# A graph network's message blocks: values woven in pairs of slots, one reduction for the maximum, and another order of the blocks

## The reference

```
msg     = relu(h[src] + edge_attr) + 1e-7
m       = msg * t
seg_max = segment_max(m, dst)
ex      = exp(m - seg_max[dst])
denom   = segment_sum(ex, dst)
agg     = segment_sum(msg * ex / denom[dst], dst)
out     = mlp(h + agg)          # 64 -> 128 -> layer norm -> relu -> 64
```

## Time and profile before

| | |
|---|---|
| median of 3 runs | 5808.66 us |
| the profiled execution, its span | 5825.41 us, 5823.0 us |
| busy in the span: PE, DVE, POOL, ACT | 81%, 78%, 69%, 34% |
| first gather of each layer at | 1686.0, 2708.5, 3732.3, 4757.7 us |
| mean granted TensorE clock | 0.868 of full |

### The profile page before, as it was taken

How to read it: one execution, slowest core, us unless ns; L and a number is a source line. 1 busy time by engine, 2 the same in 40 slices (tenths; PEclk the granted TensorE clock), 3 DMA queues, 4 the chain that set the end, 5 groups by cost and what they waited for, 6 DMA issues and landing times.

```text
span 5823.0 us, 108077 instructions
## 1 busy us (share of the span) xinstructions
PE 4692.3 (81%) x43853; PEld 3246.1 (56%) x43853; DVE 4557.1 (78%) x8649; ACT 1992.2 (34%) x3506; POOL 4032.3 (69%) x3659
## 2 busy tenths in 40 slices
PE   6727788899958888886888798688888867896887
PEld 6726677788945554553555455355545544554544
DVE  9723555654549998996999899699989968997887
ACT  3314675665523332332233223223323322222222
POOL 2433777777637777774777777477777747777775
PEclk8966987976659999998999999899999978998988
DMA  8993777775665556554555655455565545555552
GB/s 338 413 304 111 274 282 270 263 274 211 240 218 196 183 198 181 186 200 144 181 186 200 174 192 193 148 173 198 191 174 200 184 148 177 188 189 161 177 178 96
DMA packets 317390, 1192.47 MB, mean 205 GB/s; under 512 B 139314, under 2 KB 142564, under 8 KB 249556
## 3 DMA queue, kind: packets, MB, share of 16 engines
q1 hardware_dynamic: 166676, 920.68, 42.9%
q0 software_dynamic: 128800, 209.18, 14.0%
q10 hardware_dynamic: 21408, 55.60, 2.4%
HBM read 930.35 MB, written 254.82 MB: 204 GB/s over the span
## 4 chain that ended last, share of the span: by engine, by line
DVE 35%; PE 13%; POOL 10%; issue 8%; DMA 2%; ACT 2%; SPq 0%; DVEq 0%; POOLq 0%
POOL gb L1285 9%; PE bank L1394 9%; DVE ep_layers L1384 5%; DVE xb L1318 5%; DVE ep_layers L1345 5%; DVE ep_layers L1370 4%; DVE ep_layers L1340 4%; PE bank L1302 2%; DMA gb<-ztab,ovi 2%; DVE xb L1328 1%; DVE ds L1404 1%; DVE na L1431 1%; ACT hb L282 1%; DVE st L254 1%; PE bank L1448 1%
## 5 line engine op out<-in xcount | busy, mean ns | idle before, releaser
L1285 POOL DMA_INDIRECT gb<-ztab,ovi x2512 | 2794.2, 1112 | 869.5 <-issue 736.3
L1394 PE MATMUL bank<-ep_layers,keep 128*128 128x512 f32 (+3 forms) x4928 | 2248.6, 616 | 43.2 <-DVE ep_layers L1384 43.2
L1394 PEld LDWEIGHTS bank<-ep_layers,keep 128*128 128x128 f32 x4928 | 995.9, 205 | 1241.1 <-issue 1181.8
L1302 PE MATMUL bank<-zpw,oh_layers 128*128 128x64 bf16 x28812 | 880.8, 194 | 104.2 <-DMA zpw<-ztab 104.1
L1302 PEld LDWEIGHTS bank<-zpw,oh_layers 128*128 128x128 bf16 x28812 | 874.4, 98 | 159.0 <-issue 137.1
L1131 POOL DMA_INDIRECT ecell<-zpw,ptg x588 | 627.3, 1067 | 227.8 <-issue 175.6
L1376 ACT ACTIVATE ep_layers<-ep_layers,pack 128x1280 f32<-128x1280 f32 (+14 forms) x484 | 641.9, 1347 | 190.1 <-DVE ep_layers L1370 183.9
L1370 DVE SCALAR_TENSOR_TENSOR ep_layers<-xb,bank 128x1280 f32<-128x1280 f32 (+14 forms) x484 | 689.2, 1468 | 6.8
L1384 DVE SCALAR_TENSOR_TENSOR ep_layers<-xb,ep_layers 128x1280 f32<-128x1280 f32 (+14 forms) x484 | 687.0, 1469 | 0.4
L960 PE MATMUL bank<-byk,zpw 96*102 96x102 f32 (+13 forms) x4608 | 624.3, 317 | 43.2 <-DVE zpw L941 39.4
L960 PEld LDWEIGHTS bank<-byk,zpw 96*102 96x102 f32 (+13 forms) x4608 | 609.4, 224 | 58.5 <-DVE zpw L941 49.2
(11 more groups left out here) (219 smaller groups left out, 4697.2 us busy)
## 6 DMA issues: line engine op xcount, KB each, us to landing
oh_layers<-ohd SPq DMA_DIRECT2D x196, 1568.0 KB
cb<-rowc SPq DMA_DIRECT2D x49, 1152.0 KB
ea_in<-in_ea SPq DMA_DIRECT2D x101, 512.0 KB, 9.3
enc<-es_out ACTq DMA_DIRECT2D x101, 512.0 KB
gb<-ztab,ovi POOLq DMA_INDIRECT x2512
ohd<-oh_lay SPq DMA_DIRECT2D x49, 736.0 KB
xb<-ecell SPq DMA_DIRECT2D x20, 1536.0 KB
xb<-ecell SPq DMA_DIRECT2D x20, 1504.0 KB
```

The costliest lines, as they stand in the source:

```text
L1285: at["g"][d] = ga_l[d % GB_BLOCKS](GP.indirect_dma_start(gb[:, c:c + 64], None, from_rows, bass.IndirectOffsetOnAxis(ap=ovi[:, i:i + 1], a ...
L1302: q = PE.matmul(gps[j % n_gp][:, 64 * (s % 8):64 * (s % 8) + 64], oh[:, d % 2, at_oh:at_oh + 128], zp[:, b, 64 * part:64 * part + 64], sta ...
L1394: q = PE.matmul(both[:, 0:w], ident, rows[:, 128 * (c - a):128 * (c - a) + w], start=(c == 0), stop=(c + 4 >= S.S[d]), skip_group_check=True)
```

## The change

1. A new tile `xs` ("woven" in the profile) takes the sums of `add` and `over`, instead of `xb`. Slot pairs are interleaved in it: features of a slot q of half 0 and a slot q of half 1 stand next to each other (`half(t, a, b)` is one of the two, with a step of two elements). `over` is cut in two where it crosses the halves; where S is odd a memset fills the missing slot.
2. `most` is one `tensor_reduce` over pairs and slots, into `mx`, and one `tensor_scalar` (maximum with 0) into `top_x`; ACT applies its own relu before its exp for `cm`.
3. `sub` and `mul` read `xs`, in slices that each lie in one half, of at most 28 slots. One block has four slices, and its fourth `sub` comes behind its first `mul`. `xb` is free after `over`, and `add(d, 0)` waits for the last `mul`.
4. The order: V = 7, 6, 6, 5, then 13, 16, 13, 15, 13, 15, 12 ... 13, 11, 36, 11, 21, 11, 20, 10, 19 ... 16, 9, 16, 9, and 8, 8, 8, 7 at the end. The block of 36 stands at place 25, and its `gb_after` is 24. `prepare` scatters nodes by their plain rank and reads them back with five strided DMAs, instead of computing the places with nine small operations.

```diff
-        self.turn = self.ND // 2
-        ends = [d // 2 if d % 2 else self.ND - 1 - d // 2 for d in range(self.ND)]
-        self.sorted = ends[self.turn:] + ends[:self.turn]
+        few, half = self.ND - 8, (self.ND - 9) // 2
+        self.runs = [(0, 1, few + 4, 4), (4, 2, half, few - half), (5, 2, half // 2, half - half // 2),
+                     (5 + 2 * (half - half // 2), 2, 0, half // 2), (self.ND - 4, 1, few, 4)]
+        at = {p + step * i: b + i for p, step, b, n in self.runs for i in range(n)}
...
+            def half(t, a, b):
+                return xs[:, 128 * a:128 * b].rearrange("p (q f t) -> p t q f", t=2, f=64)[:, t]
...
-                k["add"][d] = V(VE.tensor_tensor(x, gps[j % n_gp][:, 0:64 * (hi - lo)], x,
-                                                 ALU.add))
+                if j == 0 and "read" in link:
+                    vwait(link["read"])
+                t, q = place[j]
+                k["add"][d] = V(VE.tensor_tensor(
+                    half(t, q, q + hi - lo), by_slot(gps[j % n_gp][:, 0:64 * (hi - lo)]),
+                    by_slot(x_of(d, lo, hi)), ALU.add))
...
-                q = V(VE.tensor_tensor(row[:, 0:64 * m], x_of(d, 0, m), x_of(d, n - m, n), ALU.max))
-                yield
-                while m > 2:
-                    vwait(q)
-                    w = m // 2
-                    q = V(VE.tensor_tensor(row[:, 0:64 * w], row[:, 0:64 * w],
-                                           row[:, 64 * (m - w):64 * m], ALU.max))
-                    m -= w
...
-                q = k["topx"][d] = V(VE.scalar_tensor_tensor(
-                    top, row[:, 0:64], 0.0, row[:, 64:128], ALU.max, ALU.max))
-                vwait(q)
-                q = k["topx"][d] = V(VE.tensor_copy(top_x[:, d % 2, :], top))
+                q = V(VE.tensor_reduce(top, xs[:, 0:128 * halves(d)[0]].rearrange(
+                    "p (q f t) -> p f q t", t=2, f=64), AX.XY, ALU.max))
+                yield
+                vwait(q)
+                q = k["topx"][d] = V(VE.tensor_scalar(top_x[:, d % 2, :], top, 0.0,
+                                                      None, ALU.max))
...
                 for i in range(n):
                     mul(d, i)
+                    if i + EP_SLICES < n:
+                        sub(d, i + EP_SLICES)
```

More of the change, by code:

```diff
@@ L62, in __init__ @@
         assert self.ones[-1] == self.ND and self.G == 36
-        self.turn = self.ND // 2
-        ends = [d // 2 if d % 2 else self.ND - 1 - d // 2 for d in range(self.ND)]
-        self.sorted = ends[self.turn:] + ends[:self.turn]
+        few, half = self.ND - 8, (self.ND - 9) // 2
+        self.runs = [(0, 1, few + 4, 4), (4, 2, half, few - half), (5, 2, half // 2, half - half // 2),
+                     (5 + 2 * (half - half // 2), 2, 0, half // 2), (self.ND - 4, 1, few, 4)]
+        at = {p + step * i: b + i for p, step, b, n in self.runs for i in range(n)}
+        self.sorted = [at[d] for d in range(self.ND)]
+        assert sorted(self.sorted) == list(range(self.ND))
         self.place = [self.sorted.index(b) for b in range(self.ND)]
@@ L1248, in x_of, with by_slot, halves @@
                 return xb[d % 2][:, 64 * a:64 * b]
-            def slices(d):
-                n = -(-S.S[d] // EP_SLOTS)
-                w = 4 * -(-S.S[d] // (4 * n))
-                return [(a, min(S.S[d], a + w)) for a in range(0, S.S[d], w)]
+            def half(t, a, b):
+                return xs[:, 128 * a:128 * b].rearrange("p (q f t) -> p t q f", t=2, f=64)[:, t]
+            def by_slot(t):
+                return t.rearrange("p (q f) -> p q f", f=64)
+            place = [(0, 0), (0, 8), (1, 0), (1, 8), (0, 16)]
+            def halves(d):
+                return -(-S.S[d] // 2), S.S[d] // 2
+            def slices(d):
+                cuts = []
+                for t, m in enumerate(halves(d)):
+                    n = -(-m // EP_SLOTS)
+                    w = 4 * -(-m // (4 * n)) if n > 1 else m
+                    cuts += [(t, a, min(m, a + w)) for a in range(0, m, w)]
+                return cuts
             ring_of, ring_user = {}, []
@@ L1261, in ring @@
                 return ring_of[d, i] % EP_SLICES
-            def wait_ring(d, i):
-                n = ring_of[d, i]
-                if n >= EP_SLICES:
-                    VE.wait_ge(pe_s, k["sums"][ring_user[n - EP_SLICES]])
             def load_x(d):
@@ L1326, in over @@
                 awaits(VE, at["g"][d])
-                x = x_of(d, G, S.S[d])
-                k["over"][d] = V(VE.tensor_tensor(x, gb[:, 64 * S.gb_at[d]:64 * (S.gb_at[d] + S.V[d])], x, ALU.add))
+                row = gb[:, 64 * S.gb_at[d]:64 * (S.gb_at[d] + S.V[d])]
+                m = halves(d)[0] - 20
+                for t, q, a, b in ((0, 20, 0, m), (1, 16, m, S.V[d])):
+                    if b > a:
+                        k["over"][d] = link["x_free"][d % 2] = V(VE.tensor_tensor(
+                            half(t, q, q + b - a), by_slot(row[:, 64 * a:64 * b]),
+                            by_slot(x_of(d, G + a, G + b)), ALU.add))
+                if S.S[d] % 2:
+                    m = halves(d)[1]
+                    V(VE.memset(half(1, m, m + 1)[:, 0], 0.0))
             def most(d):
-                vwait(max(k["over"][d], k["add"][d]))
+                vwait(V.n)
                 top = mx[:, 64 * (d % 2):64 * (d % 2) + 64]
@@ L1380, in mul @@
             def mul(d, i):
-                a, b = slices(d)[i]
+                t, a, b = slices(d)[i]
                 r = ring(d, i)
                 VE.wait_ge(ae_s, k["exp"][d, i])
-                k["mul"][d, i] = link["x_free"][d % 2] = V(VE.scalar_tensor_tensor(
-                    ep[:, r, 0:b - a, 64:128],
-                    x_of(d, a, b).rearrange("p (s f) -> p s f", f=64), 0.0,
-                    ep[:, r, 0:b - a, 0:64], ALU.max, ALU.mult))
+                k["mul"][d, i] = link["read"] = V(VE.scalar_tensor_tensor(
+                    ep[:, r, 0:b - a, 64:128], half(t, a, b), 0.0, ep[:, r, 0:b - a, 0:64],
+                    ALU.max, ALU.mult))
                 PE.wait_ge(ve_s, k["mul"][d, i])
@@ L1394, in mul @@
                     q = PE.matmul(both[:, 0:w], ident, rows[:, 128 * (c - a):128 * (c - a) + w],
-                                  start=(c == 0), stop=(c + 4 >= S.S[d]),
+                                  start=(i == 0 and c == a),
+                                  stop=(i == len(slices(d)) - 1 and c + 4 >= b),
                                   skip_group_check=True)
@@ L1613, in layer @@
                 steps(99, "end" if ready else "turned")
-                for i in range(1 if ready else 0, n):
+                for i in range(1 if ready else 0, min(n, EP_SLICES)):
                     sub(d, i)
```

54 lines of the change are left out of this document (18 added, 36 removed).

## The result

The changed kernel takes 5985.07 us (median of 4 runs, 5975.22 to 5987.5) and the one before 5811.2 (5808.57 to 5826.21): 1.0291 times as long, 95% interval 1.0269 to 1.0312. I had forecast 5736. The profiled execution took 5987.5, its span is 5985.1.

The account below looks back on a forecast made before the run. DVE and POOL were taken to run level, both full and coupled through delayed gathers. Layer terms of -4, -14, -14 and -41 us made -73, so 5808.7 - 73 = 5736 us, range 5685 to 5835.

Parts of the forecast that it names:

- The maximum: In `most` on DVE: one reduction and a small operation take 3.51 us instead of 4.42, saving 44.6 us a layer.
- DVE's work: DVE's net change over a whole layer, from the shorter reduction, additions, slices and waits for PE: -30 us a layer.
- The block with four slices: Its fourth `sub` must wait for PE's sums behind its first `mul`: +4.4 us a layer on DVE.
- What POOL gets back: Gathers on POOL, no longer delayed by the tree of maxima, get back 60 us a layer, bounds 0 and 75.
- the first rival: The reduction delays POOL's gathers as long as the tree did, so POOL gets nothing back: 5861 us, chance 0.09.
- What is added on DVE: Split `over`, memset and two new waits on DVE cost 0.23 us a block, 11 a layer.
- hand-offs: First `add` waiting for last `mul`, 0.06 us, and reduction waiting for everything before, 0.05; bounds 0 and 0.2 each.
- The order: New block order changes DVE's waits for gathers by +26, +16, +16 and -11 us in the four layers.
- start waits: First two `over` of a layer wait 3.98 and 5.77 us; fewer early gathers save 9.7 in layers two and three.
- the pairs cost POOL what they cost DVE, +3: Behind the block of 36, alternating blocks of about 20 and 10 gathers cost only 3 us.
- the waits that exist grow, +5: DVE's existing waits for PE grow 5 us a layer, as the shorter maximum takes 0.9 of 2 us slack.
- What would show it wrong: Wait at block of 36 above 45 us or missing, gathers staying at 1.1 us, or DVE awaiting PE every block.

## Why the prediction was wrong

I had forecast 73 us less; it became 174 us more. The runs at full pace make a table: medians in us, those of before 5810.73 to 5818.51 in the same jobs.

| | order of before | new order |
|---|---|---|
| tree, its own steps | 5811 to 5819 (before) | 5967.81 |
| woven, two steps | 5696.8 | 5848.09 |
| woven, one step | 5828.46 | 5985.07 (the change) |

Each part has about the same price wherever the table has it twice: the woven tile and reduction -122 and -120, the order +151 to +157, the lost step +132 and +137. -122 + 151 + 137 = +166, measured +174. The lost step beside the tree has no run at full pace.

- **The maximum.** The size was right: 3353 ns for 3072 columns, forecast 3.35 us. The way to it was partly luck. I called the two rows of my slope contiguous, but `fold` (684 ns for 512 columns) adds four sums that lie 128 columns apart in PSUM; the contiguous row alone (1953 ns for 1728, 1.13 a column) would have given 3.47. I had forecast DVE's work at -30 us a layer; its busy time is down by 27 in the second layer and 30 in the last. The woven tile with its reduction, by itself, is worth 120 to 122 us of time.
- **The block with four slices** waits 29.6 us over four layers, forecast 17.6.
- **What POOL gets back.** The mean of a gather is 1042 ns, forecast near 1.02, so 70 of 1112 - 940 = 172 ns: 44 us a layer instead of 60. The direction holds: the first rival fell. What it is worth in time no run separates.
- **The step that failed first: "What is added on DVE"**. I counted the instructions that the change adds and not what it takes from the schedule around them. `most` is a place where the node stage is issued, and with the second yield gone one cast on ACT moved behind an exp. Nothing in the rows of before shows such a wait (4.4 us in 12 times). The nearest term of the forecast is that for hand-offs, 11 us a layer within 0 and 30, and it stood for other waits; the lost step costs 137 us, and its waits are all in the three layers that write rows, 44.6 us in each.
- **The step that failed second: "The order"**. I priced it by gathers alone: +26, +16, +16 and -11 us of waits, 47 in all. That part came, near enough: waits for gathers are 147.0 us where those figures add up to 37 + 37 + 37 + 54 = 165, with 34.8 us at the block of 36 (forecast 33) and none of the start waits. But the order's price is 151 us. Between the two kernels with two steps the waits show where: +74 for linear2, +50 for gathers, +26 for the rows of the residual input, together 150. I had written "the pairs cost POOL what they cost DVE, +3" and "the waits that exist grow, +5" for PE, and never asked which of a pair's two blocks the residual add follows. The place costs 132 us in the new order (up to 36 of them can be the block of 36) and 32 in the order of before, where only 11 pairs have it and the two blocks of a pair differ less on the whole. With the places right in both (and the block of 36 two places ahead in the new order), the new order costs 5716 - 5665 = 51 us more, close to the 47 that I had for it (by the waits 36 for gathers and 18 for the residual rows): the gathers were priced near enough, the pair was not priced at all. The wait of `h` for linear2, 31.1 us in 29 times, was in the trace of before.
- **The sum.** -73 was made of -120, +47 and nothing for the other two. With the measured 137 for the step and 151 for the order it would have been -120 + 137 + 151 = +168.
- **What would show it wrong.** "If DVE waits for PE in every block" came true in kind: DVE waits for linear2 88 times in 100 node units, that is in nearly every pair of blocks. PE's waits at `fold` stayed below the 25 us, read as a layer's like the figures around it: 43.7 us in four layers, 10.7 in the second where before has 14.1. PE's longer leg showed at linear2 and not where I looked for it.
- **The layers.** The first lost 71 us, the second and third 52 and 50, the last gained 7. In each of the first three the cast wait grew by 43 us and the wait for linear2 by 28 to 30. The first layer's waits for gathers grew by 24 us and the second's by 14, since the first had no start waits to lose, as forecast; that is 10 of the 19 us between them. In the last layer there is no cast wait, and waits for gathers fell from 64.7 to 41.8 us, forecast 54.

## What to carry to other kernels

Where instructions of two stages are interleaved by hand, a `yield` is part of the cost of the code that holds it: when five operations become one, count the places at which the other stage was issued, and follow what it issues there to the queues of all engines. When an order is changed for one engine, write down a pair's instructions on each engine under both orders and look at which large operation stands ahead of the one that is waited for. And test the parts of a change apart: here one part gained 2.2%, two lost 2.6% and 2.3%, and keeping the good one and putting right the order gave 0.9755 of the time.

## What the runs showed of the hardware

- A reduction over pairs of fp32 that lie together, 512 bytes from pair to pair, runs at 1.09 ns a column; one column in 196 bytes ran at 1.82.
- Gathers are shorter with the reduction than with the tree (mean 1042 against 1112 ns; those beside a reduction 0.94 to 0.98 us); that agrees with the rule of the Trainium skill ("SBUF — State Buffer", Who interferes with whom) weighed in the prediction.
- In the pairs shown TensorE's granted clock fell to 0.50 behind an idle piece of 4.7 us and stayed at 1.00 behind one of 2.1 us. The length of the piece alone doesn't decide: with the places exchanged the clock stayed at 1.00 behind one of 3.21 us (transpose at 3630.37 us), and linear1 fell to the lower rate behind one of 1.59 us (transpose at 2338.02 us).
- In 12 of 18 runs small matmuls were issued at 126 ns instead of 34, the whole run long. The idle time before them is "issue", for which the trace has no releaser. The kernel before then takes 1.52 to 1.55 times as long, so it is not the kernel's doing; chips 12 and 15 each had one run at either pace, so it is not the chip alone. What sets the pace is not shown.
